# Grouped attention with its turns and projections a batch ahead, the query stacks turned in two halves

## The reference

```python
D, H, KVH, HD, LAT, WIN = 128, 16, 4, 8, 32, 32
def global_latent_attn(x, wq, w_kv_down, w_k_up, w_v_up, wo):
    q = split_heads(x @ wq, H)
    latent = x @ w_kv_down
    k, v = split_heads(latent @ w_k_up, KVH), split_heads(latent @ w_v_up, KVH)
    q, k = qk_norm(rope(q, BASE_G)), qk_norm(rope(k, BASE_G))
    k, v = repeat_kv(k), repeat_kv(v)
    return merge_heads(sdpa(q, k, v, causal)) @ wo
# local_gqa_attn: the same with k = x @ wk, v = x @ wv, and a mask of 0 <= i - j < 32
```

## Time and profile before

| | |
|---|---|
| median of 3 runs | 2553.79 us (2549.93 to 2562.5) |
| profiled execution | 2568.21 us, its span 2566.4 us |
| TensorE busy in the span | 2127.1 us (83%) |
| VectorE, ScalarE busy | 1467.1 us (57%), 1001.0 us (39%) |
| mean granted TensorE clock | 0.860 |

### The profile page before, as it was taken

One profiled execution on the slowest core, in us unless ns is written; L12 is line 12 of the kernel. 1 busy time (PEld: TensorE's weight loads), 2 busy tenths in 40 slices (PEclk: granted clock), 3 DMA queues, 4 the chain that ended last, 5 costly groups with the idle time before them and its releaser, 6 DMA issues. The chain is left out here.

```text
span 2566.4 us, 40401 instructions
## 1 busy us (share of the span) xinstructions
PE 2127.1 (83%) x13860; PEld 1681.5 (66%) x13860; DVE 1467.1 (57%) x3930; ACT 1001.0 (39%) x2247; POOL 131.4 (5%) x191
## 2 busy tenths in 40 slices
PE   3578788669995884899799989999889987688876
PEld 1455455459992222899799958888689984455543
DVE  6644354655667998566522237777632228555537
ACT  1245344332222330222344445555444435234334
POOL 1100000110001001000000000000000000000000
PEclk9778677769997996899799989999989989566658
DMA  5000000000000000000000024433300000000000
GB/s 155 7 1 1 1 1 1 29 1 1 0 0 1 0 1 0 34 0 0 1 1 0 0 83 128 123 123 123 97 1 0 0 1 0 1 1 0 0 1 16
DMA packets 47126, 59.75 MB, mean 23 GB/s; under 512 B 7089, under 2 KB 44689, under 8 KB 46323
## 3 DMA queue, kind: packets, MB, share of 16 engines
q1 hardware_dynamic: 47023, 58.43, 7.4%
HBM read 32.20 MB, written 26.21 MB: 23 GB/s over the span
## 5 line engine op out<-in xcount | busy, mean ns | idle before, releaser
L701 ACT ACTIVATE m2a_hid<-psum,m_b 128x256 f32<-128x256 f32 x256 | 100.2, 474 | 114.7 <-PE psum L55 114.6
L701 ACT ACTIVATE m2b_hid<-psum,m_b 128x256 f32<-128x256 f32 x256 | 100.3, 474 | 113.9 <-PE psum L55 113.9
L686 PE MATMUL psum<-m_w,m2a_hid 128*128 128x128 f32 x1024 | 126.2, 278 | 0.0
L686 PE MATMUL psum<-m_w,m2b_hid 128*128 128x128 f32 x1024 | 125.8, 277 | 0.0
L719 DVE SCALAR_TENSOR_TENSOR m2b_acc<-psum,m2b_gates,m2b_acc 128x128 f32<-128x128 f32 x128 | 39.0, 346 | 147.9 <-PE psum L686 147.9
L719 DVE SCALAR_TENSOR_TENSOR m2a_acc<-psum,m2a_gates,m2a_acc 128x128 f32<-128x128 f32 x128 | 39.0, 346 | 147.3 <-PE psum L686 147.3
L686 PEld LDWEIGHTS psum<-m_w,m2a_hid 128*128 128x128 f32 x1024 | 122.2, 194 | 0.6
L686 PEld LDWEIGHTS psum<-m_w,m2b_hid 128*128 128x128 f32 x1024 | 121.8, 194 | 0.6
L2050 ACT ACTIVATE a_p<-a_p,a_nmax 128x256 f32<-128x256 f32 x128 | 64.0, 500 | 141.7 <-DVE a_nmax L2077 141.7
L1793 DVE TENSOR_REDUCE a_nmax<-psum 128x2 f32<-128x512 f32 x128 | 82.9, 687 | 48.7 <-PE psum L1634 48.6
L1056 DVE TENSOR_TENSOR_SCAN a1s_clamped<-a1s_clamp_coef,a1s_bounds 128x1024 f32<-128x1024 f32 x48 | 108.6, 2265 | 0.0
(11 more groups left out here) (608 smaller groups left out, 5687.6 us busy)
## 6 DMA issues: line engine op xcount, KB each, us to landing
a_scratch<-a_pos SPq DMA_DIRECT2D x64, 384.0 KB, 2.7
a_shifted<-a_scratch SPq DMA_DIRECT2D x64, 256.0 KB, 3.1
m_w<-in_m_w SPq DMA_DIRECT2D x1, 2048.0 KB
arena<-in_m_w SPq DMA_DIRECT2D x1, 2048.0 KB, 8.8
arena<-in_m_up SPq DMA_DIRECT2D x1, 1760.0 KB, 7.6
a_w<-in_a_w SPq DMA_DIRECT2D x1, 1536.0 KB, 7.5
out<-X SPq DMA_DIRECT2D x1, 1024.0 KB, 5.1
m_down<-in_m_down SPq DMA_DIRECT2D x1, 880.0 KB
```

The costliest lines, as they stand in the source:

```text
L686: last = nc.tensor.matmul(ps_y(e % 2)[:, t * D:(t + 1) * D], hid[:, e % 2, c * SEQ + t * P:c * SEQ + (t + 1) * P], m.m2_w2[:, e, c, :], st ...
L701: last = nc.scalar.activation(hid[:, e % 2, c * SEQ:(c + 1) * SEQ], ps_up(e % 2)[:, c * SEQ:(c + 1) * SEQ], ACT.Gelu, bias=m.m2_b1[:, e * ...
```

## The change

The query stacks are turned in two halves of four transposes, both into bank 5, each copied to `qT` by ScalarE before the next is turned (`turn_queries`, `qsT_ready`). So bank 4 is no longer used for stacks, and the turn of the stacks no longer waits for `y_used`; the turn of the tokens does. The turn of the tokens and the latent (`start_a`, `start_b`) go from groups 0 and 1 of the batch before to groups 6 and 7 of the batch before that, and the projection, now `start_c` in both stages, goes to group 0. On VectorE `start_d` goes from group 3 to 1, `start_d2` from 4 to 3, `end_c` from 5 to 4, the input's statistics from 6 to 2 and `start_b` from 7 to 4.

```diff
@@ TensorE
+                if not isinstance(n, int) or n > 2:
+                    pe.wait_ge(y_used, n - 2)
...
+            def turn_queries(u, n, half):
+                for j in range(2):
+                    for t in range(PAIR):
+                        heads = slice(KV * (2 * half + j), KV * (2 * half + j + 1))
+                        last = nc.tensor.transpose(m.psum[:, 5, j * SEQ + t * P:j * SEQ + (t + 1) * P],
+                                                   qs[:, t, heads, :].rearrange("p h f -> p (h f)").bitcast(F32), m.ident[:, :])
+                last.then_inc(qsT_ready, 1)
+
             def start_d(u, n):
                 pe.wait_ge(qk_ready, n + 1)
+                turn_queries(u, n, 0)
                 if not isinstance(n, int) or n:
                     pe.wait_ge(o_ready, 4 * n - 3)
-                if not isinstance(n, int) or n > 1:
-                    pe.wait_ge(y_used, n - 1)
...
+            def start_e(u, n):
+                pe.wait_ge(qT_ready, 2 * n + 1)
+                turn_queries(u, n, 1)
...
-                    if g < 3 and next:
-                        (start_a, start_b, start_c)[g](1 - u, n + 1)
+                    if g == 0 and next:
+                        start_c(1 - u, n + 1)
...
                     if g == 5 and next:
                         start_d(1 - u, n + 1)
+                    if g == 6 and next:
+                        start_e(1 - u, n + 1)
+                    if g == 6 and later:
+                        start_a(u, n + 2)
+                    if g == 7 and later:
+                        start_b(u, n + 2)
@@ ScalarE
-                    if g == 6 and next:
-                        start_e(1 - u, n + 1)
+                    if g in (5, 6) and next:
+                        start_e(1 - u, n + 1, g - 5)
+                    if g == 6 and later:
+                        start_b(u, n + 2)
+                    if g == 7 and later:
+                        start_c(u, n + 2)
@@ VectorE
-                    if g in (0, 2) and prev:
-                        normalise(1 - u, n - 1, 2 + g // 2)
+                    if g == 0 and prev:
+                        normalise(1 - u, n - 1, 2)
+                    if g == 1 and next:
+                        start_d(1 - u, n + 1)
+                    if g == 2 and prev:
+                        normalise(1 - u, n - 1, 3)
+                    if g == 2 and later:
+                        start_a(u, n + 2)
                     if g == 3 and next:
-                        start_d(1 - u, n + 1)
-                    if g == 4 and next:
                         start_d2(1 - u, n + 1)
                     if g == 4:
                         normalise(u, n, 0)
-                    if g == 5 and prev:
+                    if g == 4 and later:
+                        start_b(u, n + 2)
+                    if g == 4 and prev:
                         end_c(1 - u, n - 1)
                     if g == 5 and next:
                         start_e(1 - u, n + 1)
...
-                    if g == 6 and later:
-                        start_a(u, n + 2)
...
-                    if g == 7 and later:
-                        start_b(u, n + 2)
```

More of the change, by code:

```diff
@@ L1223, in start_b, with start_c @@
                 else:
+                    pass
+            def start_c(u, n):
+                if not isinstance(n, int) or n:
+                    pe.wait_ge(qT_ready, 2 * n)
+                if local:
                     for t in range(PAIR):
@@ L1226, in start_b @@
                     last.then_inc(p_ready, 1)
-            def start_c(u, n):
-                if not local:
+                else:
                     pe.wait_ge(latT_ready, n + 1)
@@ L1306, in first @@
                 start_d(0, 0)
+                start_e(0, 0)
+                start_a(1, 1)
+                start_b(1, 1)
                 ready(0)
@@ L1363, in start_d, with start_e @@
                 nc.scalar.activation(inv[:, :], inv[:, :], ACT.Exp, scale=-0.5).then_inc(ssinv_ready, 1)
[L1365 to L1369, removed]
+            def start_e(u, n, half):
+                act.wait_ge(qsT_ready, 2 * n + half + 1)
+                nc.scalar.activation(qT[:, u, 2 * half:2 * half + 2, :].rearrange("p j f -> p (j f)"), m.psum[:, 5, :], ACT.Copy).then_inc(qT_ready, 1)
             def exps(u, n, g):
@@ L1387, in first @@
                 start_d(0, 0)
-                start_e(0, 0)
+                start_e(0, 0, 0)
+                start_e(0, 0, 1)
+                start_b(1, 1)
+                start_c(1, 1)
             def unit(u, n, prev, next, later):
@@ L1392, in unit @@
                     exps(u, n, g)
-                    if g == 0 and next:
-                        start_b(1 - u, n + 1)
                     if g == 1 and prev:
                         move_values(1 - u, n - 1, 3)
-                    if g == 1 and next:
-                        start_c(1 - u, n + 1)
                     if g in (3, 5, 7):
                         move_values(u, n, g // 2 - 1)
+                    if g == 3 and next:
+                        start_d(1 - u, n + 1)
                     if g == 4 and prev:
                         end_b(1 - u, n - 1)
-                    if g == 4 and next:
-                        start_d(1 - u, n + 1)
-                    if g == 6 and next:
-                        start_e(1 - u, n + 1)
+                    if g in (5, 6) and next:
[4 more added lines that the diff above has]
+                        start_c(u, n + 2)
             def tail(u, n):
@@ L1535, in unit @@
             def unit(u, n, prev, next, later):
+                if later:
+                    norm_power(nc, pool, m, rn, n + 2)
                 if prev and local:
                     norm_power(nc, pool, m, xn, n - 1)
-                if later:
-                    norm_power(nc, pool, m, rn, n + 2)
             def tail(u, n):
```

10 lines of the change are left out of this document (5 added, 5 removed).

## The result

| | before | after |
|---|---|---|
| median, 11 runs each | 2554.92 us (2549.93 to 2570.23) | 2539.16 us (2529.75 to 2546.34) |
| profiled execution, span | 2568.21, 2566.4 us | 2546.34, 2544.6 us |
| TensorE busy | 2127.1 us (83%) | 2095.9 us (82%) |
| mean granted clock | 0.860 | 0.871 |

The ratio of after to before is 0.9922, 95% interval 0.9902 to 0.9942: faster by 0.8%. It is not the ratio of the two medians, which is 0.9938. The forecast was 2534 us, with 2517 to 2550. Both profiled executions are among the longest of their kernel: 2568.21 us of at most 2570.23, and 2546.34 us, the longest of the 11.

What follows compares the result with a forecast made beforehand. TensorE sets the pace, with one large stall per batch ahead of `start_d` that also lowers its clock. Gains of 18 us global and 2 us local, 20 together, gave 2534 us from the median 2553.8, range 2517 to 2550.

Steps and rivals of the forecast that it cites:

- The stall: TensorE's wait ahead of `start_d`, 3.21 us per global batch before; forecast to leave 0.1 to 0.2 us there.
- the 13.7: TensorE's work in a global batch at full clock, in us: 15.61 busy less 0.10 x 18.84 lost to the clock.
- Stall three: TensorE's turn-back behind `start_d` waiting for `kT`: 1.0 us in a global batch, 2.25 us in a local one.
- the 0.5 us taken off there for the clock: Local batch: 0.03 x 16.32 taken off 12.82 us of TensorE busy time, leaving 12.3 us of work.
- The global sum: Global stage: gains of 2 us at the entry, 12 in six batches, 4 in the last; 18 us together.
- All four stalls: Global batch: waits at `end_a` 1.3 us, `start_d` 0.1, `kT` 1.0, batch's end 0.9; full clock assumed.
- the wait only moves: Rival, global stage: small stalls still cost the clock, giving back 15 of the 20 us; 2549 us, chance 0.25.
- The local sum: Local stage: batches of 16.8 us at full clock and 20.3 at the lower; a gain of 2 us.
- the same alternation as before: Five local batches: three at the lower clock and two at full clock, 3 x 1.0 less 2 x 0.5 us gained.
- the rival of a full clock: Local stage at full clock throughout: five batches gain 11 us, the last about 6; 2519 us, chance 0.17.
- The forecast of 20 us: Whole kernel: total gain, 18 us from the global stage and 2 from the local one.

Runs made afterwards that it cites:

- The fillers: Kernel before, with 14 identity transposes that nobody reads on TensorE ahead of `start_d`, nothing reordered: 2531.33 us, ratio 0.9897.
- The order alone: Kernel after, but the stacks turned all at once into banks 4 and 5, behind `y_used`: 2530.5 us, ratio 0.9871 to before.
- the halves alone: Kernel before's work order, but stacks turned in halves through bank 5 and `start_d` not waiting for `y_used`: 2582.28 us, ratio 1.0087.
- The fillers of the 1.0 us stalls: Kernel after with `kT` copied before `end_c`, plus seven identity transposes ahead of `end_a` and six ahead of the next `start_b`: 2539.16 us, ratio 0.991.
- the last run: Kernel after with `kT` copied first, `end_a`, `end_b`, `start_b` later, plus six identity transposes ahead of `start_d`: 2514.18 us, ratio 0.9817.
- the kernel with the long wait: Kernel after, with four further unneeded VectorE copies in the global `end_c`, ahead of `kT`'s copy: 2559.68 us, ratio 0.999 to before.

## Why the prediction was right, point by point

**The stall and what replaces it.** Right. Forecast 1.3, 0.1 to 0.2, 1.0 and 0.8 to 0.9 us in a global batch; measured 1.07, nil, 0.64 and 0.83. The batch came out at 16.97 us where 17.0 to 17.1 was said, though the stalls sum to 2.5 and not 3.3: TensorE was busy 14.43 us at a clock of 1.00, and the 13.7 worked out for that was 0.7 low. The two errors cancel, so that the batch fits to 0.1 us is luck. Stall three was put 0.36 too long. The local one, forecast at 2.25, was 2.17 once and 1.8 to 1.9 otherwise, and the local busy time was 12.96 where 12.3 was said. Part of the error is the 0.5 us taken off there for the clock. The window of that batch in the kernel before, without the stall at its end, has the whole busy time at 1.00, so the low share lay in idle time:

```profile
362.29:375.64 13.35, 12.81 (x142) 8.53 (x142) 8.16 (x34) 6.87 (x16) 1.38 (x2) 1.00 0.00 0
```

**The global sum.** Entry 2.1 us less (said 2), six batches 14.2 less (said 12: 101.82 instead of 104), the last 4.5 less (said 4): 20.8 instead of 18.

**The premise on the clock.** "All four stalls are shorter than any after which the clock fell, so I take the full clock" was not safe. It held for five of six batches. In the first, the clock reads 0.50 behind a stall of 1.07 us. TensorE's timeline:

```profile
164.80 0.44 PE L1305 MATMUL psum<-ident,global_o 128*128 128x128 f32 x2 [1.07 <-DVE global_o L1496]
```

The window just behind it:

```profile
166.00:168.00 2.00, 2.00 (x20) 0.83 (x18) 1.85 (x9) 0.81 (x1) 0.69 (x1) 0.50 0.02 4
```

The low level lasted some 3 us, and from that batch's latent to the next one's (156.18 to 173.94) it took 17.76 us, 0.8 over the others. The rival "the wait only moves" rests on the same behaviour, and on this case it was far closer than a chance of 0.25 sounds: with stall three at 2.1 in place of 0.64 the whole gain was gone (the ratio of 0.999).

**The local sum.** The 5.0 us look like the 2 that were said, but two steps failed and cancelled. A batch at full clock was forecast at 16.8 and took 16.91, a low one at 20.3 and took 20.47. "I take the same alternation as before, three such batches and two at full clock" failed: the clock fell in four of five, and the five took 98.78 us, 3.6 more than before instead of 2 less. And the last local batch, for which the forecast had nothing and only the rival of a full clock had 6, gained 7.1: it now runs at 0.90 instead of 0.50. The entry gave 1.5.

**Where the gain comes from.** The prediction said that what is gained is the clock. The fillers show it for the whole: with the old order and the old wait they give 0.9897. In the global stage, which gave most of the change's gain, they reach 13.5 of its 20.8 us, and there the shorter waits count beside the clock. What it did not weigh is that the two parts of the change pull apart. The order alone gives 0.9871; the halves alone cost 0.9%. Together they gain only 0.8%, because the halves let TensorE arrive at `kT` ahead of VectorE. The prediction had seen this wait and the clock's fall behind it, but priced it at half a microsecond a batch at full clock and no more falls than before; its price was the clock. VectorE's queue could not go round it: the Trainium skill, PSUM — Partial Sum Buffer, section "Engine vs sequencer instructions", has it first in, first out, and the trace agrees, `kT` being copied at 343.50 behind the statistics of 342.35. Putting it ahead by hand gives 0.9845.

**The size.** The forecast of 20 us was 21.8 in the spans, and 15.8 in the medians. One execution of each kernel doesn't fix a gain that hangs on where the clock falls: the runs of after spread over 16.6 us.

**Open.** What makes the clock fall behind one stall of about 1.0 or 1.9 us and not behind the next of the same length wasn't settled, nor whether one stall's length or the idle time of several together counts: a filler changes both. The fillers of the 1.0 us stalls made a longer wait of their own in the local stage, and the last run told too little.

## What to carry to other kernels

Price a stall of the engine whose clock can fall by the low stretch behind it, not by its own length: here 1.5 us more of waiting in at most seven batches cost 28.7 us in the trace. Look at the engine that releases the wait before moving work on the one that waits; one line moved in VectorE's queue was worth as much as the whole reordering. Transposes that nobody reads, put into the wait, tell in one run how much of a stall's price is the clock. And when a change has two parts, time each alone, since here one lost part of what the other had won.

## What the runs showed of the hardware

In the steady attention batches of these traces the granted clock fell behind every stall of TensorE of 2.0 us or more that began at the full clock. Of twelve of 1.80 to 1.92 us it fell behind eight (in the kernel after at 361.01, 381.45 and 402.16, not at 344.07; in the kernel before at 399.89, not at 362.29 and 420.10), and it fell behind some of 1.0 to 1.3. The low level then lasted between 3 and some 20 us although TensorE was busy nearly all of it: 17.38 of 18.00 us at 0.50, from 194.50 on, in the kernel with the long wait. At the entry of the local stage it could last longer: with the halves alone TensorE was busy 18.99 of 20.00 us from 320.00 on, all of them at 0.50. Transposes of the identity that nobody reads kept the clock at 1.00 as well as useful work did, for 81.77 us on end of the local stage; in the global one, behind stalls of 1.33 us, the clock fell in two batches of six all the same. The kernel with 14 transposes more in each batch, 1.75 us of them, was 1.0% faster.
